# Attention scores from 32-row groups of TensorE, without a separated copy of the keys, and the routing of a batch in three parts

## What is computed

```python
def _L1_xattn_ref(query, key, value, mask, Wq, bq, Wk, bk, Wv, bv, Wo, bo):
    q = _split_heads(query @ Wq + bq)      # (4, 16, 256, 8)
    k = _split_heads(key @ Wk + bk)
    v = _split_heads(value @ Wv + bv)
    scores = jnp.einsum('bhqd,bhkd->bhqk', q, k) / jnp.sqrt(jnp.float32(DK))
    scores = jnp.where(mask[:, None, :, :] == 0, jnp.float32(-1000000000.0), scores)
    p_attn = jax.nn.softmax(scores, axis=-1)
    x = jnp.einsum('bhqk,bhkd->bhqd', p_attn, v)
    ...
def _L1_ffn_ref(hidden_states, w_red, wg, W1, b1, W2, b2):
    logits = x_red @ wg_n.T
    gates = jax.nn.softmax(logits, axis=1)
    scores = jnp.max(gates, axis=1)
    idx = jnp.argmax(gates, axis=1)
    ...
```

## Time and profile before

| | us |
|---|---|
| median of 3 runs | 248.2 (247.9 to 248.48) |
| profiled execution, whole | 249.16 |
| its span, first to last instruction | 247.3 |
| mean granted clock of TensorE, share of full speed | 0.952 |

### The profile page before, as it was taken

One profiled execution on the slowest core, in us unless ns is written; L12 is line 12 of the kernel. 1 busy time (PEld: TensorE's weight loads), 2 busy tenths in 40 slices (PEclk: granted clock), 3 DMA queues, 4 the chain that ended last, 5 costly groups with the idle time before them and its releaser, 6 DMA issues.

```text
span 247.3 us, 4771 instructions
## 1 busy us (share of the span) xinstructions
PE 192.6 (78%) x1750; PEld 134.4 (54%) x1750; DVE 173.2 (70%) x454; ACT 135.4 (55%) x271; POOL 119.1 (48%) x231
## 2 busy tenths in 40 slices
PE   0479865998328479776989988988897895999994
PEld 0358653897203177552433543543555784798883
DVE  4678888994684979869767786886755655739252
ACT  2246744939476578435767567667794256260100
POOL 8131768996649857831587784784221022000000
PEclk9999999999955789998899999999999997999999
DMA  5895040000000000000000000000000000000000
GB/s 169 324 398 219 0 170 4 0 4 0 3 1 0 0 0 3 3 3 3 0 0 5 1 0 3 0 3 0 3 1 3 0 0 4 0 3 21 24 21 21
DMA packets 4461, 8.75 MB, mean 35 GB/s; under 512 B 514, under 2 KB 3026, under 8 KB 4052
## 3 DMA queue, kind: packets, MB, share of 16 engines
q1 hardware_dynamic: 3636, 7.78, 8.4%
q10 hardware_dynamic: 800, 0.63, 0.8%
HBM read 7.89 MB, written 0.52 MB: 34 GB/s over the span
## 4 chain that ended last, share of the span: by engine, by line
PE 31%; POOL 29%; DVE 19%; issue 9%; ACT 7%; DMA 2%; SPq 1%; POOLq 0%; DVEq 0%
PE ps L1252 28%; POOL gate_pt L514 6%; POOL rstd L380 5%; POOL w L400 3%; PE ps L1261 3%; POOL x_in L431 3%; DMA wf<-weights_dram 2%; POOL w L392 2%; POOL vareps L377 2%; DVE gate_pt L1033 2%; DVE mx L1090 2%; DVE amax L1027 2%; DVE stats L798 2%; DVE half_c L1080 2%; ACT gate_pt L758 1%
## 5 line engine op out<-in xcount | busy, mean ns | idle before, releaser
L1090 DVE TENSOR_REDUCE mx<-ps 128x2 f32<-128x512 f32 x64 | 42.2, 686 | 16.6 <-PE ps L1252 16.5
L758 ACT ACTIVATE gate_pt<-ps 128x512 f32<-128x512 f32 x64 | 37.2, 603 | 15.6 <-PE ps L1252 15.3
L1252 PE MATMUL ps<-w,hid_xm 128*128 128x256 f16 (+1 forms) x288 | 30.3, 263 | 0.1
L514 POOL TENSOR_SCALAR gate_pt<-ka_mem 32x256 f16<-32x256 f16 x64 | 25.5, 399 | 4.4
L1252 PE MATMUL ps<-gate_pt,half_c 128*128 128x512 f16 x64 | 25.0, 393 | 3.2 <-issue 1.9
L1252 PEld LDWEIGHTS ps<-w,hid_xm 128*128 128x128 f16 x288 | 25.4, 101 | 3.4 <-issue 0.4
L1252 PE MATMUL ps<-qb,gate_pt 128*128 128x256 f16 x128 | 25.4, 281 | 0.8
L1261 PE MATMUL ps<-cst,rows 128*128 128x128 f32 x32 | 7.5, 333 | 18.0 <-ACT rows L662 8.8
L1252 PE MATMUL ps<-gate_pt,hid_xm 128*32 128x256 f32 x256 | 20.4, 390 | 1.5 <-ACT gate_pt L758 1.5
L1252 PEld LDWEIGHTS ps<-qb,gate_pt 128*128 128x128 f16 x128 | 9.5, 99 | 18.7 <-issue 11.4
L380 POOL TENSOR_TENSOR rstd<-vareps,halfs 128x2 f32<-128x2 f32 x24 | 17.7, 738 | 2.0
(11 more groups left out here) (221 smaller groups left out, 505.6 us busy)
## 6 DMA issues: line engine op xcount, KB each, us to landing
stage<-weights_dram SPq DMA_DIRECT2D x2, 1024.0 KB, 11.1
wf<-weights_dram SPq DMA_DIRECT2D x4, 256.0 KB, 8.5
wf<-mask_dram SPq DMA_DIRECT2D x1, 1024.0 KB, 4.8
eb_oT<-ffw_dram SPq DMA_DIRECT2D x1, 768.0 KB, 8.2
ctx_in<-ctx_rows_dram ACTq DMA_DIRECT2D x4, 128.0 KB, 5.9
x_in<-x_dram SPq DMA_DIRECT2D x4, 128.0 KB, 3.1
gate_pt<-ctx_cols_dram SPq DMA_DIRECT2D x1, 512.0 KB, 8.5
out_dram<-ctx_in SPq DMA_DIRECT2D x4, 128.0 KB, 1.7
```

The source lines that it names most:

```text
L514: ins = nc.gpsimd.tensor_scalar(kz[part, n % KRING, k], ka[part, b, quad], 1.0, 0.0, ALU.mult, ALU.add)
L758: nc_act(pt[:, head % PRING].rearrange("p t n -> p (t n)"), ps[:, 2 + head % 2, :], ACT.Exp, scale=DK ** -0.5).then_inc(sig["probs"], 1)
L1090: V.tensor_reduce(mx[:, b, head:head + 2, t], score_bank(4 * n + i).rearrange("p (h n) -> p h n", h=2), AX.X, ALU.max).then_inc(sig["smax" ...
L1252: return nc.tensor.matmul(dst, lhsT, rhs, start=start, stop=stop, skip_group_check=True)
```

## The change

- `kz`, its clearing and `separated_keys` are gone from POOL.
- A plain instruction is now one head and one half of the queries: 32 rows of `qa` as weights, 32 rows of `ka` as moving data, 256 columns. A head is two of them, in one bank, and DVE's maximum is taken over the 2 halves of one head, again 128x512. PLAIN_HEADS gives the order of the heads, so that the plain head lies two row groups from the shifted head beside it.
- A shifted instruction takes 32 rows of `ka` as weights and 32 rows of `qb` as moving data, 256 columns.
- The four matmuls of a place alternate: shifted, plain, shifted, plain. Both waits (`probs` and `smax`) stand ahead of the four.
- The halves of the weighted values stand at k = 0 and k = 2.
- The logits step stands at place 12 instead of 13, and DVE's choice is cut into three parts at places 12, 13 and 14, with a maximum between them.

```diff
-KRING = 4
+PLAIN_HEADS = (2, 3, 0, 1)
...
 TAIL_START = 22
-TAIL_STEPS = (0, 2, 4, 6, 10, 13, 15)
+TAIL_STEPS = (0, 2, 4, 6, 10, 12, 15)
 TAIL_ROWS = 9
+ROUTE_AT = (12, 13, 14)
 POOL_ROOTS = (7, 11)
...
-        kz = taken(gate_pt, PRING * TILES * T, KRING * 4 * T // 2).bitcast(F16).rearrange(
-            "p (r h n) -> p r h n", r=KRING, h=4)
...
-            pool.wait_ge(sig["kscale"], 1)
-            nc.gpsimd.memset(kz[:, :, :, :], 0.0).then_inc(sig["zeros_ready"], 1)
...
-            def separated_keys(n):
-                b, quad = divmod(n, QUADS)
-                pool.wait_ge(sig["ka_ready"], B + b + 1)
-                if n >= KRING:
-                    pool.wait_ge(sig["st_mm"], 4 * (n - KRING + 1))
-                for k in range(4):
-                    part = slice(32 * k, 32 * k + 32)
-                    ins = nc.gpsimd.tensor_scalar(kz[part, n % KRING, k], ka[part, b, quad], 1.0, 0.0, ALU.mult, ALU.add)
-                ins.then_inc(sig["kz_ready"], 1)
-
-
-            pool.wait_ge(sig["zeros_ready"], 3)
+            pool.wait_ge(sig["zeros_ready"], 2)
             pool.wait_ge(sig["ln_rstd"], nth_norm(LN_ATT, B - 1))
-            for n in range(KRING):
-                separated_keys(n)
-            pool.wait_ge(sig["kz_ready"], KRING)
             shift_rows(0)
             shift_rows(1)
             for n in range(B * QUADS):
@@ -528,10 +511,6 @@
                     rows_shift(LN_MOE, POOL_ROOTS.index(n))
                 if n + 2 < B * QUADS:
                     shift_rows(n + 2)
-                if n + KRING < B * QUADS:
-                    pool.wait_ge(sig["spread"], n + 3)
-                    separated_keys(n + KRING)
-                    pool.wait_ge(sig["kz_ready"], n + KRING + 1)
                 if n < 3:
                     router_part(2 * n)
...
@@ -1084,10 +1063,9 @@
 
             def head_max(n, i):
                 b, quad = divmod(n, QUADS)
-                t, pair_of = divmod(i, 2)
-                head = 4 * quad + 2 * pair_of
+                head = 4 * quad + PLAIN_HEADS[i]
                 dve.wait_ge(sig["s_mm"], 4 * n + i + 1)
-                V.tensor_reduce(mx[:, b, head:head + 2, t], score_bank(4 * n + i).rearrange("p (h n) -> p h n", h=2),
+                V.tensor_reduce(mx[:, b, head, :], score_bank(i).rearrange("p (t n) -> p t n", t=TILES),
                                 AX.X, ALU.max).then_inc(sig["smax"], 1)
 
 
...
-
+            def route(b, part):
+
+                if part == 0:
                     dve.wait_ge(sig["logit_mm"], b + 1)
-                    V.tensor_copy(logits[:, b], tb[:, 0:TILES * NE].rearrange("p (t e) -> p t e", t=TILES))\
+                    V.tensor_copy(logits[:, b], tail_bank(b)[:, 0:TILES * NE].rearrange("p (t e) -> p t e", t=TILES))\
                         .then_inc(sig["logits"], 1)
                     dve.wait_ge(sig["logits"], b + 1)
                     for t in range(TILES):
                         ins = V.max(top8[:, b, t], logits[:, b, t])
                     ins.then_inc(sig["top8"], 1)
+                if part == 1:
                     dve.wait_ge(sig["top8"], b + 1)
                     V.tensor_scalar(ntop[:, b], top8[:, b, :, 0], -1.0, None, ALU.mult)
                     for t in range(TILES):
                         ins = V.max_index(topix[:, b, t], top8[:, b, t], logits[:, b, t])
                     ins.then_inc(sig["topix"], 1)
+                if part == 2:
                     dve.wait_ge(sig["topix"], b + 1)
                     for t in range(TILES):
                         ins = V.tensor_scalar(onehot[:, b, t], c("iota"), topix[:, b, t, 0:1], None, ALU.is_equal)
                     ins.then_inc(sig["onehot"], 1)
-
 
             def masked_tokens(b):
                 dve.wait_ge(sig["oh"], 2 * b + 2)
@@ -1160,8 +1140,11 @@
                     if n + 2 < B * QUADS:
                         head_max(n + 2, k)
                     now, before = tail_at(n, k), tail_at(*divmod(4 * n + k - 1, 4))
-                    if now and now[1] not in (2, 4):
+                    b, place = tail_place(n, k)
+                    if now and now[1] in (0, 1, 3):
                         tail_dve(*now)
...
+                    if 0 <= b < B - 1 and place in ROUTE_AT:
+                        route(b, ROUTE_AT.index(place))
                     if before and before[1] in (2, 4):
                         tail_dve(*before)
                     if (n, k) == (B * QUADS - 1, 0):
@@ -1218,7 +1201,8 @@
             pair_masks(0)
             pair_masks(1)
             tail_dve(3, 0)
-            tail_dve(2, 5)
+            for part in range(3):
+                route(2, part)
             tail_dve(3, 1)
             gates(0)
             gates(1)
...
@@ -1467,23 +1452,36 @@
                     ins = column_bias(dst, "bq", k)
                 ins.then_inc(sig["q_mm"], 1)
 
-            def scores(n, i, masked):
+            def rows_of(k):
+
+                return slice(32 * k, 32 * k + 32)
+
+            def scores_wait(n, i):
 
                 b, quad = divmod(n, QUADS)
-                t, pair_of = divmod(i, 2)
                 if n == 0 and i == 0:
                     pe.wait_ge(sig["qa_ready"], 1)
-                if i == 0:
-                    pe.wait_ge(sig["kz_ready"], n + 1)
+                if quad == 0 and i == 0:
+                    pe.wait_ge(sig["ka_ready"], B + b + 1)
                 if 4 * n + i >= 2:
                     pe.wait_ge(sig["smax"], 4 * n + i - 1)
-                dst = score_bank(4 * n + i)
-                ins = mm(dst, qa[:, b, quad, t * P:(t + 1) * P],
-                         kz[:, n % KRING, 2 * pair_of:2 * pair_of + 2].rearrange("p h n -> p (h n)"), True, not masked)
+
+            def scores_tile(n, i, t, masked):
+
+                b, quad = divmod(n, QUADS)
+                head = rows_of(PLAIN_HEADS[i])
+                dst = score_bank(i)[:, t * T:(t + 1) * T]
+                ins = mm(dst, qa[head, b, quad, t * P:(t + 1) * P], ka[head, b, quad], True, not masked)
                 if masked:
-                    for h in range(2):
-                        ins = mm(dst[:, h * T:(h + 1) * T], idbig[:, :], resmask[:, b, t], False, h == 1)
-                ins.then_inc(sig["s_mm"], 1)
+                    ins = mm(dst, idbig[:, :], resmask[:, b, t], False, True)
+                if t == TILES - 1:
+                    ins.then_inc(sig["s_mm"], 1)
+
+            def scores(n, i, masked):
+
+                scores_wait(n, i)
+                for t in range(TILES):
+                    scores_tile(n, i, t, masked)
 
             def shift(n):
 
@@ -1495,23 +1493,36 @@
                     mm(ps[:, 6, t * P:(t + 1) * P], spread[:, n % 2, t], id16[:, :], t == 0, False)
                 mm(ps[:, 6, 0:T], id16[:, :], qa[:, b, quad], False, True).then_inc(sig["shift_mm"], 1)
 
-            def shifted_scores(n, k, masked):
-
-                b, quad = divmod(n, QUADS)
+            def shifted_wait(n, k):
+
                 head = 4 * n + k
                 if k == 0:
                     pe.wait_ge(sig["qb"], n + 1)
                 if head >= 2:
                     pe.wait_ge(sig["probs"], head - 1)
-                for t in range(TILES):
-                    tok = slice(t * P, (t + 1) * P)
-                    dst = ps[:, 2 + head % 2, t * T:(t + 1) * T]
-                    ins = mm(dst, kz[:, n % KRING, k, tok], qb[:, n % 2], True, not masked)
-                    if masked:
-                        for q in range(TILES):
-                            ins = mm(ps[:, 2 + head % 2, t * T + q * P:t * T + (q + 1) * P],
-                                     resmask[:, b, q, tok], idbig[:, :], False, q == TILES - 1)
-                ins.then_inc(sig["st_mm"], 1)
+
+            def shifted_tile(n, k, t, masked):
+
+                b, quad = divmod(n, QUADS)
+                tok = slice(t * P, (t + 1) * P)
+                dst = ps[:, 2 + k % 2, t * T:(t + 1) * T]
+                ins = mm(dst, ka[rows_of(k), b, quad, tok], qb[rows_of(k), n % 2], True, not masked)
+                if masked:
+                    for q in range(TILES):
+                        ins = mm(dst[:, q * P:(q + 1) * P], resmask[:, b, q, tok], idbig[:, :], False, q == TILES - 1)
+                if t == TILES - 1:
+                    ins.then_inc(sig["st_mm"], 1)
+
+            def shifted_beside_plain(n, k, masked):
+
+                shifted_wait(n, k)
+                plain = n + 2 < B * QUADS
+                if plain:
+                    scores_wait(n + 2, k)
+                for t in range(TILES):
+                    shifted_tile(n, k, t, masked)
+                    if plain:
+                        scores_tile(n + 2, k, t, masked)
 
             def weighted_values(n, t):
 
@@ -1608,17 +1619,15 @@
                         shift(0)
                 for n in range(B * QUADS):
                     for k in range(4):
-                        shifted_scores(n, k, masked)
-                        if n + 2 < B * QUADS:
```

(6 more changed lines are left out.)

6 lines of the change are left out of this document (3 added, 3 removed).

## The result

The kernel became slower. Its median is **259.38 us** (256.86 to 262.72, 4 runs) beside 248.34 us (247.9 to 249.67, 4 runs) for the kernel before on the same chip: a ratio of **1.041**, 95% interval 1.035 to 1.047. The forecast was 241.8 us, with a range of 238.5 to 249.5. The profiled execution of after is the slowest of its four, 262.72 us, and is left out of the ratio; in the others the mean granted clock of PE was 0.85 to 0.87 instead of 0.842.

The account below looks back on a forecast made before the run. No engine bounds the whole; a plain quad's path is PE's up to head 2, then ACT's. Gains 5.2 - 1.1 + 2.3 (POOL) + 0.8 - 0.8 = 6.4 us, so 248.2 becomes 241.8 us, range 238.5 to 249.5.

Parts of the forecast that it names:

- PE's clock stays at 1.00 in the loop: Loop of 14 quads: PE's blocks were all priced at the upper clock level; a fall stood only in rival (d).
- rival (d): PE's clock falls in the loop with less work, 0.9 us more a quad; four quads give 245, twelve 252; chance 0.04.
- rival (b): Row groups don't run side by side: a head stays at 0.44 us, in all 247.4 us (246 to 249); chance 0.12.
- rival (a): Loads of a pair's second shifted matmul don't hide: 0.2 us a quad, 2.8 in all, about 245 us; chance 0.12.
- rival (c): Tiling changes on PE are dear: gain gone at 0.19 us each, 252 us in all at 0.25; chance 0.12.
- The plain quad: Quad without a tail step: 3.33 us against 3.70, 0.37 saved in each of 14 quads, 5.2 us in all.
- POOL's spreads: PE's three waits for POOL's spreads, 1.7 us, go without separated keys; 1.0 us gained net (bounds 0 and 1.7).
- ACT's rows: PE's waits for ACT's rows, 3.1 us in two places, shrink with less POOL work: 1.3 us gained (bounds 0 and 3.1).
- - 1.1: Eight tail steps fall on k = 2 where nothing is spare, each losing 0.14 us: 1.1 us lost.
- Routing in parts: Maxima and scores no longer stand still for DVE's 1.2 us block, twice: 0.4 us each, 0.8 gained.
- The new order of waits: Awaiting `smax` ahead of the shifted head delays an exponential twice, 0.4 us each: 0.8 us lost.
- Rival (e): More waits go than counted, POOL's upper bounds and both routing blocks in full: 4 us more, 237.5 us; chance 0.06.

Follow-up runs that it names:

- e7: e5 with 1, 1, 0 and 1 extra matmuls behind heads 0 to 3 instead of 2, 1, 0 and 2: 249.41 us (244.87 to 256.04).
- e1: The changed kernel with the plain head in the row group of the shifted head beside it, so pairs can't run side by side: 284.54 us, one run.
- e14: e1 plus unused whole-array matmuls ahead of the loop, to start it at the upper clock: 285.53 us, one run.
- e4: The changed kernel with the separated keys and 128-row score matmuls back, new order and routing in parts kept: 250.24 us, ratio 1.0075 to the kernel before.
- e8: e5 with the halves of the weighted values at k = 0 and 1, as before the change: 256.01 us (249.06 to 263.03).
- e6: e5 with the routing in one block and the logits at place 13, as before the change: 246.8 us, ratio 0.9935 to the kernel before.
- e15: The kernel before with only the routing changed: logits at place 12, DVE's choice in three parts: 249.22 us, ratio 1.0039.
- e5: e3 without the extra matmuls behind a head that a tail step follows: 249.38 us, ratio 1.0034 to the kernel before.
- e10: e6 with both shifted matmuls first and the wait for smax behind them, as before the change: 246.53 us, ratio 0.9915 to the kernel before.
- e13: e10 with extra matmuls also behind heads whose tail step waits for another engine: 246.95 us, ratio 0.9936 to the kernel before.
- e3: The changed kernel plus unused whole-array matmuls ahead of the loop and five a quad within it (2, 1, 0, 2 behind heads 0 to 3): 247.88 us, ratio 0.9957.
- e9: e3 with the loop's extra matmuls on 32 of 128 rows, those ahead of the loop left whole: 254.06 us, one run.

## Why the prediction was wrong

**The step that failed is that PE's clock stays at 1.00 in the loop.** All of PE's terms in the sum were priced at the upper level; the fall stood only in rival (d), with a chance of 0.04 and a price of 0.9 us a quad. It came in twelve of the 14 quads, at 1.6 in a plain one (4.93 in after against 3.30 in e7). The 14 quads of after's profile take 15.8 us more than those of e7's (72.4 and 56.6); on the forecast of 241.8 that makes 257.6, and measured were 259.4.

Three things were wrong in (d). Its cause: the clock was to fall since PE has less work, and in e1 and e14 it falls with as many columns one after the other as before. The reason against it: that the last two quads were idle for 2.1 of 12.1 us and stayed at 1.00 compared busy shares only. Those quads' matmuls of scores used all 128 rows; after's use 32, and e14 against e4 shows that this decides: from 1.00 to 0.50 after 3.71 of 4 us busy, and 1.00 with 2.21 of 4. And its price, which counted two blocks on the path; at 0.50 nearly all of PE's work is on the path, since ACT then waits for PE 2.3 us a quad.

The Trainium skill (TensorE: Matmul & The Clock Gate, What's actually happening) has activity of PE release its clock, and says that the chip goes by how busy PE has been. A reader would take the profile's busy share for that, as the forecast did. Here the traces differ: e14's share is above e4's, and its clock is half.

**What held.** Row groups run side by side, so rival (b) is out: pairs are 0.12 us apart, and a head takes 0.24 as forecast. Loads hide, which answers rival (a): the second pair follows the first by 0.12, no more than its columns. A change of tiling is 0.10 (forecast 0.10), so rival (c) is out. The plain quad is 3.29 in e7, forecast 3.33, and that with three extra matmuls. That it comes so close is partly luck: the exponential of head 2 starts 0.27 behind the copy, not 0.38; head 3 is late by 0.29, not 0.11, of which the extra matmul behind head 1 makes 0.12; and the next weighted values start 0.65 behind head 3's own exponential, not 0.76. Moving the weighted values, part of that quad, is worth 0.33 in plain quads (e8). POOL's spreads: PE's loads wait for them once in after, 0.4 us, where it was three times and 1.7, and POOL's busy time in the loop fell by 19.4 us. The wait for ACT's rows, part of the 1.3 us taken for them, did not shrink in after, and at the upper clock (e6) from 3.1 to 2.2. Waits of after, for the first line of the earlier trace rows:

```profile
PEld ps L1246 <- ACT rows L595: 3.1, 2, 1.9
```

**The loop without the clock's fall.** The profile of before is not a fair match for the first quads, since its clock was 0.70 and 0.80 in two of them; e15, with the plain and shifted scores of before, had 1.00 throughout. The periods again, all at 1.00:

| kernel | quads 0 to 5 | quads 6 to 13 | the 14 |
|---|---|---|---|
| e15 | 2.85 3.07 3.98 4.23 3.75 3.69 | 4.43 4.91 5.36 4.55 4.07 4.91 5.36 5.13 | 60.3 |
| e7 | 3.23 3.17 3.30 3.30 3.30 3.30 | 4.26 4.75 4.43 5.04 4.30 4.75 4.43 5.04 | 56.6 |
| e6 | 3.34 3.27 3.52 3.51 3.51 3.51 | 4.36 4.75 4.43 4.28 4.61 4.75 4.43 4.28 | 56.6 |

The first six quads take 19.6 us in e7 and 21.6 in e15: 2.0 saved, where 6 x 0.37 = 2.2 and 1.0 for POOL's spreads were forecast. Quads 4 and 5 give 0.42 in the mean, a little more than the 0.37; quads 2 and 3, which waited for spreads, 0.8 more than that together; quads 0 and 1 lose 0.5, and why is open. The last eight take 37.0 in e7 against 38.0 in before, and 35.9 in e6, with the routing in one block. The forecast for them, routing apart, was 8 x 0.37 - 1.1 + 1.3 for ACT's rows - 0.8 for the order of the waits, or 2.4; e6 gave 2.1. So at the upper clock plain and tail quads gave about what was counted; what is missing are the first two quads and the routing.

**Routing in parts**: forecast 0.8 gained, measured 1.0 lost alone (e15), 1.5 in the loop beside row groups (e5 against e6). The sign was wrong. The step that failed is "PE's wait for it stays about as it is": it grew from 1.1 to 1.6 us in e15. Beside row groups a second wait came, which the sum did not have: PE's for the low part at the logits step, 1.1 us. **The new order of waits**: forecast 0.8 lost; e10 against e6 shows nothing outside the intervals.

**Behind the loop**: 60.8 us against 60.3, the forecast being no change. With the extra matmuls the first of the last two quads takes 5.07 us (e6) against 4.66 in before, which nothing in the sum stood for. The 1.0 us by which after's loop begins later (115.24 against 114.23) is within what profiled executions of these kernels differ in: from 113.7 (e7) to 116.9 (e5).

Put together: with a clock that stays up and the routing in one block the change is worth some 1.5 us (e6, e10, e13), extra matmuls included; these cost 0.22 us a plain quad from three to five (e7 against e6). 244.87, the best single execution of e7, shows that more is there, but not how to hold it. Of the forecast's 6.4 us, the 0.8 of the routing was a loss, the first two quads lost 0.5, and the clock took the rest and more. In the loop e6 gains 3.0 us (0.9 in the first six quads against e15, 2.1 in the last eight), so half of it is lost again outside, where only the 0.4 above is accounted for. (Rival (e)'s bounds add up to 237.7, not 237.5; nothing rests on it.)

## What to carry to other kernels

Before whole-array matmuls are replaced by matmuls on a few rows, ask what keeps PE's clock up. A busy share near 1 does not show that it will stay: look for 0.50 in the granted clock of the first stretch after the change, and price every block of PE at the lower clock in the rival. Where the clock falls and PE has spare time, a few whole-array matmuls whose result nobody reads can be worth more (11.5 us here, e3) than the work that they add.

## What the runs showed of the hardware

- PE's clock fell from 1.00 to 0.50 after 4 us in which PE was busy for 3.71, with 32-row matmuls for the scores (e14), and stayed at 1.00 through 4 us with 2.21 busy when the scores used 128 rows (e4). Between the two, one program held the clock in some executions and not in others (e7: 0.906 to 0.962, 244.87 to 256.04 us). It can rise again on 32-row matmuls with extra ones among them: 0.65 from 120 to 124 us and 1.00 from 124 to 128 (e9).
- At either level a pair of 32-row matmuls in different row groups costs PE one: 0.12 us for 256 columns at 1.00 (e7), 0.19 at 0.50 (after). Four in four row groups started within 0.02 us (after, 123.98).
- A matmul in another row group starts ahead of an earlier one that waits for its own row group (e10, 0.11 us; in after the first pair of head 0 starts 0.17 ahead of the second pair of head 3). So the order in which an engine's instructions are written is not the order of these starts. The Trainium skill (TensorE: Matmul & The Clock Gate, The mechanism) has matmuls start strictly in program order; the trace of e10 differs.
- The `onehot` comparison takes 0.22 us at its shortest, and 0.88 for two of them beside a product of POOL that started at 154.19 and took 1.16 (e5). Whether POOL is the cause was not tried.
